# First weights, first rows and the tile search ahead of the branch: a perceiver block on one Trainium2 core

## The chip, the core and the metric

The kernel runs on one core of a Trainium2 chip. A core has five engines that run their own instruction lists and meet at semaphores: PE (TensorE, products), DVE (VectorE), ACT (ScalarE), POOL (GpSimd) and SP (SyncE, which here only issues transfers). Transfers between memory and the core run on DMA queues. The metric is the device time of one launch in microseconds (us): before the change 1093.79 us, the median of three runs that lay between 1090.33 and 1094.54.

## The reference

There are 32 items of 64 rows of width 512 (`x`), and for each a context of 1601 rows with a mask that marks the rows past the item's length. Three blocks follow each other, each on a layer norm of `x` and added to it:

```python
# 1. cross attention, 4 query heads, one key/value head of width 128; the query's rows are rms-normed again
xn, mn = rmsnorm(layernorm(x), rms_scale), rmsnorm(ctx, rms_scale)
q = rope(xn @ q_w) * 128 ** -0.5 ; k = rope(mn @ kv_w[0]) ; v = mn @ kv_w[1]
x = x + softmax(where(mask, q @ k.T, -2.38e38)) @ v @ out_w      # True keeps a context row
# 2. causal self attention, 16 heads of width 32
x = x + attn(layernorm(x), WQ, WK, WV, WO)
# 3. feed forward 512 -> 2048 -> 512, both weights rounded to -1, 0, 1; gelu and a layer norm between
x = x + (layernorm(gelu(layernorm(x) @ q(W_fc).T)) * ln_w + ln_b) @ q(W_proj).T
```

`mask` is True for the padding at the end of an item's context, and the reference keeps just the True rows, so of 1601 context rows an item needs 400 at most. Factors `1 + rms_scale` are folded into `q_w` and `kv_w`.

## The kernel before

**A plan, then a branch.** Context rows come in tiles of 128. `plan_tiles` finds for each item which tiles hold kept rows: transfers bring the mask to the core, DVE reduces it per tile, forms running sums and from them, per item, four row offsets, a flag (`pl[4]`: the kept rows fit four tiles) and a count of tiles. Beside it the mask's rows are gathered by an indirect transfer on POOL (L153) and stored as `kept_mask`. All five engines read `onepath` and branch: to `few` (four tiles an item, taken with these inputs) or to `every`.

**Which queue does what ahead of the branch.** SP issues the loads of the first operands (`dma0`, L311): the identity, both halves of `kv_w`, `rms_scale` (element by element), the first 128 rows of `x`, the four heads of `q_w`, two tables. All transfers of the search stand on ACT's queue (L115), the store of `kept_mask` too, and ACT branches behind it.

**Behind the branch.** `few` writes its instructions by a table of slots: each stage is entered with a slot and an order in it (`at`), and the slots are run off in order, which fixes each engine's list. Every list is worked off strictly in order. Products of full precision are made from two parts: the operand rounded (hi, by ACT) and the remainder (lo, by DVE), three products each; so weights are first scaled and split (L382 on ACT, L384 on DVE). For each pair of items, `stage_Q0` normalizes 128 rows of `x` (statistics on DVE L607 and L608, two inverse square roots on POOL L262 to L615), `stage_Q1` applies it (DVE L620), `stage_Q1b` transposes and splits it, `stage_Q2` forms the queries (12 products of 128x512, called Q2 below) with the rotary factors on DVE, `stage_Q3` transposes them. For each context tile k, T(k) is its transposes (PE L220) with their split (ACT L231, DVE L234), and KV(k) the 12 products of 128x256 that follow (PE L245).

**The order that matters here.** On PE: the transposes of the first rows, Q2, T(0), T(1), the transposes of Q, T(2), KV(0), T(3), KV(1), T(4), KV(2), T(5), KV(3), then the transposes of the second pair's normalized rows, T(6), KV(4). On DVE the statistics of the second pair's rows stand ahead of the remainder of tile 3. On POOL the bias of item 0, made from `kept_mask` (L669), stands ahead of the inverse square roots of the second pair. On SP, behind the branch: for items 0, 1 and 2 four context tiles and four tables each (24 transfers, the row offset of each context tile read from `picked`), then the second pair's rows of `x`, then `kept_mask` (both L196). Below, this sequence on SP is the train.

Of the kernel before, what the change touches and what calls it, by code (L numbers as in the profile page):

```python
# [7 lines left out]
F32 = mybir.dt.float32  # L8
# [3 lines left out]
I32 = mybir.dt.int32  # L12
# [20 lines left out]
class Sem:  # L33

    def __init__(self, handle):
        self.h, self.n = handle, 0
# [48 lines left out]
def plan_tiles(nc, handle, base, mask, tmask, kmask, places, seq, plan, picked, onepath):  # L86
# [4 lines left out]
    Q = Queues()  # L91
    sems = {}

    def sem(name):
        if name not in sems:
            sems[name] = Sem(handle(name))
        return sems[name]

    op = Q.op
# [11 lines left out]
    pl = tile("pl", [6], I32, 4)  # L111
# [5 lines left out]
    D_ = lambda f, waits=(): op("dve", f, sem("p_dve"), waits)  # L117
    P_ = lambda f: op("pool", f, sem("p_pool"))
    P_(lambda e: e.memset(mk[0:B, 0:128], 0))
    z = P_(lambda e: e.memset(mk[0:B, NT * 128:], 0))  # L120
    dma(mk[0:B, 128:NT * 128], mask[:, LAST:])
    dma(sq[0:B, :], seq)
    t = dma(mk[0:B, 0:LAST], mask[:, 0:LAST], [z])
    P_(lambda e: e.memset(c0[0:B, 0:8], 0.0))
    z = P_(lambda e: e.memset(c1[0:B, 0:8], 0.0))
    for k in range(FT):
        z = P_(lambda e, k=k: e.memset(tn[0:B, k:k + 1], float(k)))
    tm = dma(tmask.rearrange("b t k -> b (t k)"), mk[0:B, :], [t, z])
    v = D_(lambda e: e.tensor_reduce(c0[0:B, 8:], mk[0:B, 0:1664].rearrange("p (t k) -> p t k", t=NT),
                                     AX.X, ALU.max), [t, z])  # L130
    for n in range(4):
# [21 lines left out]
    g = op("pool", lambda e: e.indirect_dma_start(  # L153
        km[:, :], None, tmask.rearrange("b t k -> (b t) k"), bass.IndirectOffsetOnAxis(pi[:, 0:1], 0)),
        sem("p_rows"), [wp, tm], 16)
# [3 lines left out]
    return Q, rows  # L159

def few(nc, handle, bank, base, x1d, x2d, x, ctxd, mask, rms, qw, kvw, ow, WQ, WK, WV, WO, Wfc, lnw, lnb,
        Wproj, cosk, sink, cosq, sinq, identd, causald, out, picked, kmask, ktab, t_rows, nb=B):
# [4 lines left out]

    def sem(name):
        if name not in sems:  # L170
            sems[name] = Sem(handle(name))
        return sems[name]

    Q, Q0 = Queues(), Queues()

# [17 lines left out]
    op = Q.op  # L193
# [62 lines left out]
    t_id = Q0.op("sp", lambda e: e.dma_start(ident[:, :], identd), sem("s_id"), (), 16)  # L256
# [65 lines left out]
    t_rt = dma0(sq_t[:, :], sinq, "s_rt")
    loaded = (len(sems), [t_id, t_wkv, t_rms, t_xq0, t_wq, t_rt])
# [2178 lines left out]
```

How the kernel before makes its waits and increments, by code:

```python
    def op(self, eng, fn, sem=None, waits=(), inc=1):  # L48
        for w in waits:
            if w is None:
                continue
            s, v = w
            if self.seen[eng].get(s, 0) < v:
                self.seen[eng][s] = v
                self.q[eng].append(lambda e, s=s, v=v: e.wait_ge(s.h, v))
        if sem is None:
            self.q[eng].append(fn)
            return None
        self.q[eng].append(lambda e: fn(e).then_inc(sem.h, inc))
        sem.n += inc
        return (sem, sem.n)
# [7 lines left out]
        def f(e):  # L69
            with e.If(when()):
                for g in fns[:-1]:
                    g(e)
                fns[-1](e).then_inc(sem.h, 1)
            with e.Else():
                e.drain().then_inc(sem.h, 1)
# [267 lines left out]
        def g(e):  # L343
            with e.If(when()):
                f(e).then_inc(s.h, 16)
            with e.Else():
                e.sem_inc(s.h, 16)
# [2076 lines left out]
        def run(name, e):  # L2424
            early.play(name, e)
            first.play(name, e)
            fits = e.value_load(onepath[0:1, 0:1], min_val=0, max_val=1)
            with e.If(fits > 0):
                short.play(name, e)
            with e.Else():
                for s, n in [rows, *loaded[1]]:
                    e.wait_ge(s.h, n)
                long.play(name, e)
```

## Time and profile before

| | |
|---|---|
| three timed runs, us | 1093.79, 1090.33, 1094.54 |
| profiled execution, us | 1089.65 |
| its span on the core, us | 1087.8 |
| busy share of the span | PE 86%, DVE 62%, ACT 46%, POOL 34% |
| mean granted TensorE clock | 0.965 |

The span runs from the first to the last instruction that the profiler sees; the 1.85 us between it and the execution's time lie around it. Times in the rows below count from the span's start. A busy share is an average: PE is 86% busy over the whole, but in the first slice of 40 (27.2 us) it does not work at all, and that stretch is the one that the change touches.

### The profile page before, as it was taken

Reading aid. Unit: us, or ns where it says so; the run is one execution under the profiler, and the core shown is the slowest. Engines: PE = TensorE matmul, PEld = TensorE weight load, DVE = VectorE, ACT = ScalarE, POOL = GpSimd, SP = SyncE. Lnnn points to the kernel's source line nnn. Section 1 sums busy time; section 2 is a strip of 40 time slices with the busy share of each in tenths; the row PEclk is TensorE's granted clock in tenths of the full one; section 3 lists DMA queues with packets and bytes.
Section 4 is the critical chain, followed back from the end, with each engine's and each line's share of the span. In section 5 each row is a group of like instructions: output and inputs, shape, how many; then the busy total and the mean of one; then the engine's idle time right before and its main releaser. Section 6 shows DMA issues by size and latency. Waiting matters only on the chain.

```text
span 1087.8 us, 22528 instructions
## 1 busy us (share of the span) xinstructions
PE 931.0 (86%) x7297; PEld 697.5 (64%) x7297; DVE 669.2 (62%) x1335; ACT 503.0 (46%) x1057; POOL 373.1 (34%) x500
## 2 busy tenths in 40 slices
PE   0898879898788888868879989998978999999995
PEld 0787757686667776657768878887754444444442
DVE  3587667766677766676266556766565447475543
ACT  2565445654455554535233233443445444556551
POOL 1354445444444444430012111221112334454533
PEclk9999999999999999979969999999988989999997
DMA  5532133221232322431355543443321202012011
GB/s 163 167 87 65 58 95 97 87 63 48 81 89 77 88 70 75 112 101 60 79 156 147 137 146 88 139 125 116 97 46 48 68 1 87 31 39 68 20 59 42
DMA packets 100608, 93.02 MB, mean 86 GB/s; under 512 B 45729, under 2 KB 62194, under 8 KB 100466
## 3 DMA queue, kind: packets, MB, share of 16 engines
q1 hardware_dynamic: 99856, 91.11, 28.9%
q8 instruction: 73, 1.20, 0.5%
q14 instruction: 69, 0.57, 0.2%
q10 hardware_dynamic: 578, 0.13, 0.1%
q0 software_dynamic: 32, 0.02, 0.0%
HBM read 74.37 MB, written 12.66 MB: 80 GB/s over the span
## 4 chain that ended last, share of the span: by engine, by line
PE 65%; DVE 14%; issue 10%; ACT 5%; ACTq 1%; DVEq 1%; POOL 1%; DMA 1%; SPq 1%; POOLq 0%
PE bank L245 44%; PE bank L1216 8%; PE bank L220 6%; PE bank L241 4%; DVE f L234 3%; DVE f L508 2%; ACT f L231 1%; DVEq L75 1%; ACTq L75 1%; PE bank L530 1%; ACT f L413 1%; DVE f L471 1%; DVE f L642 1%; DVE f L929 1%; PE bank L216 1%
## 5 line engine op out<-in xcount | busy, mean ns | idle before, releaser
L245 PE MATMUL bank<-f,f 128*128 128x256 f32 (+4 forms) x5032 | 635.4, 302 | 67.9 <-issue 26.3
L245 PEld LDWEIGHTS bank<-f,f 128*128 128x128 f32 (+3 forms) x5032 | 457.5, 162 | 195.7 <-issue 77.2
L220 PE MATMUL bank<-f,f 128*128 128x128 f32 x896 | 133.4, 280 | 60.1 <-DVE f L620 29.3
L234 DVE TENSOR_TENSOR f<-bank,f 128x512 fp32r<-128x512 f32 x211 | 140.7, 684 | 52.6 <-ACT f L231 50.6
L231 ACT ACTIVATE f<-bank 128x512 fp32r<-128x512 f32 x211 | 121.2, 592 | 85.6 <-PE bank L220 80.5
L220 PEld LDWEIGHTS bank<-f,f 128*128 128x128 f32 x896 | 103.6, 143 | 82.8 <-DVE f L620 31.1
L1194 POOL TENSOR_TENSOR f<-f,f 128x512 f32<-128x512 f32 x60 | 76.4, 1274 | 146.6 <-ACT f L1192 146.5
L1216 PE MATMUL bank<-f,f 128*128 128x512 f16 x512 | 124.9, 389 | 0.0
L1197 DVE SCALAR_TENSOR_TENSOR f<-bank,f,f 128x512 f16<-128x512 f32 x64 | 48.0, 750 | 107.0 <-ACT f L1184 73.5
L935 POOL TENSOR_TENSOR f<-f,f 128x512 f32<-128x512 f32 x32 | 33.4, 1045 | 182.8 <-DVE f L932 182.8
L469 POOL TENSOR_TENSOR f<-f,f 128x512 f32<-128x512 f32 x32 | 42.0, 1312 | 155.9 <-ACTq L75 133.2
L1216 PEld LDWEIGHTS bank<-f,f 128*128 128x128 f16 x512 | 51.0, 100 | 64.0 <-issue 6.8
L1183 ACT ACTIVATE bank<-bank 128x512 f32<-128x512 f32 x64 | 37.2, 582 | 94.9 <-PE bank L245 94.9
L264 POOL TENSOR_TENSOR f<-f,f 128x1 f32<-128x1 f32 (+1 forms) x100 | 75.0, 750 | 8.3
L262 POOL TENSOR_SCALAR f<-f 128x1 f32<-128x1 f32 (+1 forms) x100 | 21.3, 213 | 147.0 <-DVE f L839 94.4
L519 ACT ACTIVATE f<-f,f 128x512 f32<-128x512 f32 x64 | 46.3, 724 | 50.2 <-DVE f L517 40.3
L883 ACT ACTIVATE f<-bank 128x256 f32<-128x256 f32 x64 | 24.4, 382 | 80.8 <-PE bank L245 80.2
L241 PE MATMUL bank<-f,f 128*128 128x256 f32 x372 | 53.1, 290 | 7.5 <-issue 4.7
L508 DVE CUSTOM_DVE_ANT_0 f<-bank,f 128x512 f32<-128x512 f32 x64 | 44.2, 690 | 24.5 <-PE bank L245 16.5
L231 ACT ACTIVATE f<-f 128x256 fp32r<-128x256 f32 (+1 forms) x52 | 25.3, 497 | 69.8 <-DVE f L566 69.4
L241 PEld LDWEIGHTS bank<-f,f 128*128 128x128 f32 x372 | 46.6, 190 | 13.5 <-issue 13.3
L413 ACT ACTIVATE f<-f 128x512 bf16<-128x512 f32 x71 | 44.0, 620 | 3.2 <-ACT f L413 2.2
(128 smaller groups left out, 989.0 us busy)
## 6 DMA issues: line engine op xcount, KB each, us to landing
f<-in_ctx_dram SPq DMA_DIRECT2D x71, 256.0 KB, 2.8
f<-x_scratch SPq DMA_DIRECT2D x64, 256.0 KB, 3.7
f<-in_x_dram SPq DMA_DIRECT2D x32, 256.0 KB, 3.2
x_scratch<-f SPq DMA_DIRECT2D x32, 256.0 KB, 2.1
f<-in_L_ffn_W_fc_dram SPq DMA_DIRECT2D x32, 256.0 KB, 2.8
f<-in_L_ffn_W_proj_dram SPq DMA_DIRECT2D x32, 256.0 KB, 3.5
f<-in_ktab_dram SPq DMA_DIRECT2D x71, 64.0 KB, 2.0
f<-f SPq DMA_DIRECT2D x64, 64.0 KB, 2.4
```

What stands on the lines that cost most here:

```text
L220: f = lambda e, i=i, a=a: e.transpose(dst[:, i, :], a, ident[0:rows, 0:rows])
L231: return maybe("act", lambda e: e.activation(hi, src, ACT.Copy), sem(name + "_hi"), waits, when)
L234: return maybe("dve", lambda e: e.tensor_tensor(lo, src, hi.bitcast(F32), ALU.subtract), sem(name + "_lo"), waits, when)
L241: fns = [lambda e, i=i, a=a, b=b: e.matmul(dst, a, b, start=(first and i == 0), stop=(last and i == n - 1), skip_group_check=True) for i, ...
L245: f = lambda e, i=i, a=a, b=b: e.matmul(dst, a, b, start=(first and i == 0), stop=(last and i == n - 1), skip_group_check=check)
L264: return op("pool", lambda e: e.tensor_tensor(dst, tmp, mhalf[0:dst.shape[0], 0:n], ALU.pow), sem(name + "_p"), [t])
L413: done["sq"] = maybe("act", lambda e: e.activation(sq[:, :], cx[:, b % NG, t, :], ACT.Square, accum_out=ss[:, b % 4, t:t + 1]), sem("s_ss" ...
L508: to = op("dve", lambda e: e.tensor_tensor_reduce(Pm[:, b % 2, t, :], bank[NL][:, :], bias[:, b % 2, :], 1.0, -3.0e38, ALU.add, ALU.max, m ...
L519: te = op("act", lambda e: e.activation(Pm[:, u, t, :], Pm[:, u, t, :], ACT.Exp, bias=nm[:, u, t:t + 1], accum_out=den[:, u, t:t + 1]), se ...
L1194: tp = op("pool", lambda e: e.tensor_tensor(acc[:, v, 1, :], acc[:, v, 1, :], sq3[:, z, :], ALU.add), sem("f_acc2"), [ts, *tok["acc2", g]])
L1197: tl = op("dve", lambda e: e.scalar_tensor_tensor(Gl[:, y, :], gp, lsc[:, 0, f:f + 1], Gh[:, y, :], ALU.mult, ALU.subtract), sem("f_G_lo") ...
L1216: fn = lambda e, t=t, v=v, G=G: e.matmul(bank[kp[t]][:, :], G[:, y, t * 128:(t + 1) * 128], WPb[:, f, :], start=(f == 0 and v == 0), stop= ...
```

## The change

Four things, all ahead of or at the branch:

1. The search's loads go to SP's queue, first of all there; `rms_scale` and the first rows of `x` go to ACT's queue. The later transfers of the search (`places`, `pi`, the gather, `kept_mask`) are issued by POOL.
2. `plan` and its two transfers go away. DVE multiplies the plan by the identity (`dg`, 32 partitions of 32x6), PE sums over the partitions by one product with a column of ones, and DVE copies the row to `picked`.
3. Of `few`, the scaling and splitting of `kv_w` and `q_w` and the first pair's `stage_Q0`, `stage_Q1` and `stage_Q1b` stand ahead of the branch (`Q0` before the search's own steps, `Q1` behind them). These use one semaphore an engine. The +1 on `rms_scale` goes from DVE to POOL.
4. The branch waits for the search's answer alone, no longer for its transfers. `few` and `every` share semaphores whose counts go on from where the part ahead left them.

```diff
 def plan_tiles(...):
-    def dma(dst, src, waits=()):
-        return op("act", lambda e: e.dma_start(dst, src), sem("p_dma"), waits, 16)
+    load = lambda dst, src, waits=(): QA.op("sp", lambda e: e.dma_start(dst, src), sem("p_mk"), waits, 16)
...
-    w = dma(plan, pl[0:B, :], [v])
-    wp = dma(places, pn[0:B, :], [vp])
-    w = dma(picked[0:1, :], plan.rearrange("(a b) k -> a (b k)", a=1), [w, wp])
-    wp = dma(pi[:, :], places.rearrange("b (t a) -> (b t) a", a=1).bitcast(U32), [w])
+    v = D_(lambda e: e.tensor_tensor(dg[0:B, :, :], pl[0:B, :].unsqueeze(1).to_broadcast([B, B, 6]),
+                                     ident[0:B, 0:B].unsqueeze(2).to_broadcast([B, B, 6]), ALU.mult), [v, t_id])
+    w = QB.op("pe", lambda e: e.matmul(bank[0:1, 0:6 * B], one[0:B, 0:1], dg[0:B, :, :].rearrange("p b k -> p (b k)"),
+                                       start=True, stop=True), sem("p_pe"), [v, z])
+    vp = D_(lambda e: e.tensor_tensor(pn[0:B, :], num[0:B, :], sq[0:B, :], ALU.add), [v1, t])
+    w = D_(lambda e: e.tensor_scalar(picked[0:1, :], bank[0:1, 0:6 * B], 1.0, None, ALU.mult), [w])
     fits = picked[0:1, :].rearrange("p (b k) -> p b k", b=B)[:, :, 4]
-    v = D_(lambda e: e.tensor_reduce(onepath[0:1, 0:1], fits, AX.X, ALU.min), [w, tm])
+    v = D_(lambda e: e.tensor_reduce(onepath[0:1, 0:1], fits, AX.X, ALU.min), [w])
+    wp = QB.op("pool", lambda e: e.dma_start(places, pn[0:B, :]), sem("p_pl"), [vp], 16)
+    wp = QB.op("pool", lambda e: e.dma_start(pi[:, :], places.rearrange("b (t a) -> (b t) a", a=1).bitcast(U32)),
+               sem("p_pl"), [wp], 16)
...
-    rows = dma(kmask.rearrange("b (t k) -> (b t) k", t=FT), km[:, :], [g])
+    rows = QB.op("pool", lambda e: e.dma_start(kmask.rearrange("b (t k) -> (b t) k", t=FT), km[:, :]),
+                 sem("p_km"), [g], 16)
     for eng in ("sp", "act", "pool", "pe", "dve"):
-        op(eng, lambda e: None, None, [v, w])
+        QC.op(eng, lambda e: None, None, [v])
 def few(...):
+    t_rms = dma0("act", rms1[:, :], rms.rearrange("(c p) -> p c", p=128), "s_e_rms", allow_slow_non_contiguous=True)
+    t_xq0 = dma0("act", xq[:, :], xf[0:128, :], "s_e_xq")
...
-    at(-12, -1, lambda: load_xq(0))
-    at(-12, 0, lambda: stage_Q0(0))
+    side[0] = Q0
+    t_r1 = op("pool", lambda e: e.tensor_scalar(rms1[:, :], rms1[:, :], 1.0, 1.0, ALU.mult, ALU.add), sem("r1"), [t_rms])
+    load_xq(0)
+    stage_Q0(0)
+    t_kvh = scaled_hi(wkv_t, Wkvh, [t_wkv, t_r1])
+    t_qh = scaled_hi(wq_t, WQh, [t_wq, t_r1])
+    side[0] = Q1
+    stage_Q1(0)
+    t_Wkv = scaled_lo(wkv_t, Wkvh, Wkvl, [t_wkv, t_r1], t_kvh)
+    stage_Q1b(0)
+    tw1["q"] = scaled_lo(wq_t, WQh, WQl, [t_wq, t_r1], t_qh)
+    side[0] = Q
     for c in range(4):
-        at(-11, 7, lambda c=c: stage_WQ(c))
         at(5 + c, 9, lambda c=c: stage_Wo(c))
 def program(...):
         def run(name, e):
-            early.play(name, e)
-            first.play(name, e)
+            for q in (steps[0], prep[0], steps[1], prep[1], steps[2]):
+                q.play(name, e)
             fits = e.value_load(onepath[0:1, 0:1], min_val=0, max_val=1)
```

ACT's list at its start, before: nine transfers of the search, the read of `onepath` and the branch, then the scalings (f_71 is the hi part of `kv_w`, f_67 of `q_w`) and squares of context rows (f_76).

```order
L115 DMA tile_plan<-pl 32x6
L115 DMA tile_rows<-pn 32x4
L115 DMA picked<-tile_plan 1x192
L115 DMA pi<-tile_rows 128x1
L115 DMA kept_mask<-km 128x128
L2427 TENSOR_LOAD onepath
L2427 ISA x2
L2428 COMPARE_AND_BRANCH
L382 ACT_TABLE_LOAD
L382 ACTIVATE f_71<-f_99,f_108 128x256 x4
L382 ACTIVATE f_67<-f_100,f_108 128x512 x4
```

The same place now (f_110 is `rms_scale`, f_84 the first rows of `x`, f_73 and f_69 the hi parts, f_86 that of the first pair's transposed rows):

```order
L322 DMA f_110<-in_L_xattn_rms_scale_dram 128x4x1
L322 DMA f_84<-in_x_dram 128x512
L668 ACT_TABLE_LOAD
L668 ACTIVATE f_73<-f_101,f_110 128x256 x4
L668 ACTIVATE f_69<-f_102,f_110 128x512 x4
L241 ACTIVATE f_86<-bank 128x512
L2447 TENSOR_LOAD onepath
L2447 ISA x2
L2448 COMPARE_AND_BRANCH
L407 ACTIVATE f_78,f_111<-f_68 128x512 x4
```

The search's nine transfers are gone from ACT, and its scalings and the first split stand ahead of its branch.

DVE's list, from the search's first steps to the first rows' normalization, before (f_82 is the first rows of `x`, f_72 and f_68 the lo parts):

```order
L129 TENSOR_REDUCE c_52<-mk 32x13
L145 SCALAR_TENSOR_TENSOR pl<-c_52,cnt 32x1
L146 TENSOR_TENSOR pn<-num,sq 32x4
L152 TENSOR_REDUCE onepath<-picked 1x1
L2427 TENSOR_LOAD onepath
L378 TENSOR_SCALAR f_108<-f_108 128x4
L384 SCALAR_TENSOR_TENSOR f_72<-f_99,f_108,f_71 128x256 x4
L607 BN_STATS f_116<-f_82 128x6
L608 BN_AGGR f_117<-f_116 128x2
L384 SCALAR_TENSOR_TENSOR f_68<-f_100,f_108,f_67 128x512 x4
L620 TENSOR_SCALAR f_83<-f_82,f_117,f_118 128x512
```

The same steps now (f_74 and f_70 the lo parts, f_87 that of the first rows):

```order
L601 BN_STATS f_118<-f_84 128x6
L602 BN_AGGR f_119<-f_118 128x2
L128 TENSOR_REDUCE c_54<-mk 32x13
L144 SCALAR_TENSOR_TENSOR pl<-c_54,cnt 32x1
L145 TENSOR_TENSOR dg<-pl,f_51 32x192
L150 TENSOR_SCALAR picked<-bank 1x192
L152 TENSOR_REDUCE onepath<-picked 1x1
L614 TENSOR_SCALAR f_85<-f_84,f_119,f_120 128x512
L673 SCALAR_TENSOR_TENSOR f_74<-f_101,f_110,f_73 128x256 x4
L244 TENSOR_TENSOR f_87<-bank,f_86 128x512
L673 SCALAR_TENSOR_TENSOR f_70<-f_102,f_110,f_69 128x512 x4
L2447 TENSOR_LOAD onepath
```

The statistics of the first rows now stand ahead of the search's first step, and everything down to the lo part of `q_w` ahead of DVE's branch. The orders named above for PE, DVE, POOL and SP behind the branch are the same in both kernels.

## Rows read from the trace of the kernel before

**Rows 1.** The page's first part: busy us, share of the span, instructions.

```profile
PE 931.0 (86%) x7297; PEld 697.5 (64%) x7297; DVE 669.2 (62%) x1335; ACT 503.0 (46%) x1057; POOL 373.1 (34%) x500
```

**Rows 2.** Chain of waits, opening: start us, us, what.

```profile
20.33 1.28 ACT L382
...
31.91 4.51 PE bank L245 x12
```

**Rows 3.** Timeline, DVE, search: start us, us, engine, line, operation [idle before].

```profile
4.87 1.88 DVE L129 TENSOR_REDUCE c<-mk 32x13 f32<-32x1664 uint8 x1 [4.87 <-DMA mk<-in_mask_BxS_bk_dram]
...
8.52 0.15 DVE L145 SCALAR_TENSOR_TENSOR pl<-c,cnt 32x1 int32<-32x1 f32 x1
...
13.13 0.20 DVE L152 TENSOR_REDUCE onepath<-picked 1x1 int32<-1x32 int32 x1 [4.38 <-DMA picked<-tile_plan]
```

**Rows 4.** Timeline, first issues on ACT's and SP's queues.

```profile
0.73 0.42 ACTq L115 DMA_DIRECT2D mk<-in_mask_BxS_bk_dram  x1
...
2.20 0.51 SPq L311 DMA_DIRECT2D f<-n_L_xattn_rms_scale_dram  x1
2.75 0.50 SPq L311 DMA_DIRECT2D f<-in_x_dram  x1
3.29 3.23 SPq L311 DMA_DIRECT2D f<-in_L_xattn_q_w_dram  x4
```

**Rows 5.** DMA issues: KB, us to landing; the last one issued about 4.9.

```profile
f<-n_L_xattn_rms_scale_dram SPq DMA_DIRECT2D x1, 2.0 KB, 5.1
f<-in_x_dram SPq DMA_DIRECT2D x1, 256.0 KB, 5.2
f<-in_L_xattn_q_w_dram SPq DMA_DIRECT2D x1, 256.0 KB, 6.2
```

**Rows 6.** Timeline, SP behind the branch: the train's first and last transfers.

```profile
15.03 3.63 SPq L361 DMA_DIRECT2D f<-in_ctx_dram  x4
...
34.17 0.43 SPq L196 DMA_DIRECT2D f<-in_x_dram  x1
34.65 0.43 SPq L196 DMA_DIRECT2D f<-kept_mask  x1
```

**Rows 7.** DMA issues of 34 to 35 us: KB, us to landing.

```profile
f<-in_x_dram SPq DMA_DIRECT2D x1, 256.0 KB, 2.9
...
f<-kept_mask SPq DMA_DIRECT2D x1, 64.0 KB, 4.3
```

**Rows 8.** Timeline, POOL, 39 to 46 us.

```profile
39.04 0.62 POOL L669 TENSOR_SCALAR f<-f 128x512 f32<-128x512 uint8 x1 [4.35 <-DMA f<-kept_mask]
42.59 0.19 POOL L262 TENSOR_SCALAR f<-f 128x1 f32<-128x1 f32 x1 [2.93 <-DVE f L608]
...
44.94 0.19 POOL L615 TENSOR_TENSOR f<-f 128x1 f32<-128x1 f32 x1
```

**Rows 9.** Timeline, DVE, the second pair's statistics and normalization.

```profile
41.60 0.69 DVE L607 BATCH_NORM_STATS2 f<-f 128x6 f32<-128x512 f32 x1
...
45.81 0.54 DVE L620 TENSOR_SCALAR f<-f,f,f 128x512 f32<-128x512 f32 x1
```

**Rows 10.** Timeline, PE: KV(3) and KV(4).

```profile
45.26 1.68 PE L245 MATMUL bank<-f,f 128*128 128x256 f32 x12
...
47.57 1.67 PE L245 MATMUL bank<-f,f 128*128 128x256 f32 x12
```

**Rows 11.** Windows: length, busy us (instructions) of PE, PEld, DVE, ACT, POOL; PEclk; DMA; GB/s.

```profile
472.00:474.00 2.00, 0.19 (x2) 0.22 (x2) 1.60 (x5) 0.30 (x1) 0.78 (x3) 1.00 0.03 9
...
476.00:478.00 2.00, 1.62 (x6) 1.35 (x6) 1.20 (x4) 0.73 (x3) 0.00 (x0) 0.50 0.03 8
```

**Rows 12.** Timeline, PE: 12 products of 128x512 at either clock.

```profile
443.11 2.91 PE L245 MATMUL bank<-f,f 128*128 128x512 f32 x12
...
483.95 5.38 PE L245 MATMUL bank<-f,f 128*128 128x512 f32 x12 [2.30 <-DVEq L75]
```

**Rows 13.** Groups by shape: busy us, mean ns; a full-precision product of 512 columns.

```profile
L1292 PE MATMUL bank<-f,f 6*128 6x512 f32 x4 | 2.6, 790 | 0.0
```

More of the change, by code:

```diff
@@ L33, with __init__ @@
 class Sem:
[L36 to L37 removed]
+    def __init__(self, handle, begun):
+        self.h, self.n = handle, begun
 class Queues:
@@ L83, in play, with plan_tiles @@
             f(e)
-def plan_tiles(nc, handle, base, mask, tmask, kmask, places, seq, plan, picked, onepath):
-    Q = Queues()
+def plan_tiles(nc, handle, base, ident, t_id, bank, mask, tmask, kmask, places, seq, picked, onepath):
+    QA, QB, QC = Queues(), Queues(), Queues()
     sems = {}
@@ L157, in plan_tiles @@
     for eng in ("sp", "act", "pool", "pe", "dve"):
-        op(eng, lambda e: None, None, [v, w])
-    return Q, rows
+        QC.op(eng, lambda e: None, None, [v])
+    return (QA, QB, QC), rows, [sems[k].n if k in ("p_pool", "p_dve", "p_pe") else None for k in sems]
 def few(nc, handle, bank, base, x1d, x2d, x, ctxd, mask, rms, qw, kvw, ow, WQ, WK, WV, WO, Wfc, lnw, lnb,
-        Wproj, cosk, sink, cosq, sinq, identd, causald, out, picked, kmask, ktab, t_rows, nb=B):
+        Wproj, cosk, sink, cosq, sinq, identd, causald, out, picked, kmask, ktab, plan, nb=B):
@@ L167, in few @@
     sems = {}
+    Q, Q0, Q1 = Queues(), Queues(), Queues()
+    side = [Q0]
     def sem(name):
+        if side[0] is not Q and not name.startswith("s_e"):
+            return "s_e"
         if name not in sems:
-            sems[name] = Sem(handle(name))
+            sems[name] = Sem(*handle(name))
         return sems[name]
-    Q, Q0 = Queues(), Queues()
     class Region:
@@ L192, in snapshot, with op @@
         return [(s, s.n) for s in sems.values() if s.n]
-    op = Q.op
+    def op(eng, fn, s=None, waits=(), inc=1):
+        return side[0].op(eng, fn, sem("s_e" + eng) if s == "s_e" else s, waits, inc)
     def dma(dst, src, s, waits=()):
@@ L255, in few @@
     ident, mhalf = const(128), const(16)
-    t_id = Q0.op("sp", lambda e: e.dma_start(ident[:, :], identd), sem("s_id"), (), 16)
+    t_id = Q0.op("sp", lambda e: e.dma_start(ident[:, :], identd), sem("s_e_id"), (), 16)
+    steps, t_rows, begun = plan(ident, t_id)
     t_mh = op("pool", lambda e: e.memset(mhalf[:, :], -0.5), sem("s_mh"))
@@ L670, in stage_mask, with scaled_hi, scaled_lo @@
             bias[:, u, :], msk[:, u, :], -FILL, FILL, ALU.mult, ALU.add), sem("s_bias"), [t, *d("lgo", b - 2)])]
-    at(-12, -1, lambda: load_xq(0))
-    at(-12, 0, lambda: stage_Q0(0))
+    def scaled_hi(src, hi, waits):
+        return [op("act", lambda e, c=c: e.activation(hi[:, c, :], src[:, c, :], ACT.Copy, scale=rms1[:, c:c + 1]),
+                   sem("hi"), waits) for c in range(4)]
+    def scaled_lo(src, hi, lo, waits, ths):
+        for c in range(4):
+            tl = op("dve", lambda e, c=c: e.scalar_tensor_tensor(
+                lo[:, c, :], src[:, c, :], rms1[:, c:c + 1], hi[:, c, :].bitcast(F32),
+                ALU.mult, ALU.subtract), sem("lo"), [ths[c], *waits])
+        return ths[-1], tl
+    side[0] = Q0
[10 more added lines that the diff above has]
+    side[0] = Q
+    ahead = [(s, s.n) for s in sems.values()]
+    begun = [*begun, *(None if k.startswith("s_e_") else s.n for k, s in sems.items())]
     for c in range(4):
-        at(-11, 7, lambda c=c: stage_WQ(c))
         at(5 + c, 9, lambda c=c: stage_Wo(c))
@@ L1348, in few @@
     op("sp", lambda e: None, None, snapshot())
-    return Q, Q0, loaded
+    return Q, (Q0, Q1), steps, [t_rows, *ahead], begun
 def every(nc, handle, bank, base, x1d, x2d, x, ctxd, mask, rms, qw, kvw, ow, WQ, WK, WV, WO, Wfc, lnw, lnb,
@@ L2430, in run @@
             with e.Else():
-                for s, n in [rows, *loaded[1]]:
+                for s, n in ahead:
                     e.wait_ge(s.h, n)
```

91 lines of the change are left out of this document (38 added, 53 removed).

## Prediction, made before the changed kernel was run

> **What bounds the kernel now.** I read the page first: PE is the busiest engine with 86% of the span [rows 1], so what counts after the opening is when PE's steady run of products begins; everything behind it moves with it. Then the chain of waits of the opening: it does not run through PE until Q2 at 31.91, and before that it stands on ACT, whose table load comes at 20.33 because ACT has first to issue the search's last transfer and to branch [rows 2]. The timeline gives the rest in three pieces. The search: DVE starts on the mask at 4.87, has the plan at 8.52 + 0.15 = 8.67, and then waits 4.38 for the plan's way through memory, so that the answer stands at 13.33 [rows 3]. The train on SP: first context transfer at 15.03, that is 1.70 behind the answer, then the 24 transfers, the second pair's rows of `x` at 34.17 and `kept_mask` at 34.65 [rows 6]: 19.14 and 19.62 behind the train's start. And what hangs on these two: they land 2.9 and 4.3 after their issue [rows 7]; POOL makes the bias at 39.04, having waited 4.35 for nothing but `kept_mask`, and only behind it the second pair's inverse square roots [rows 8]; these release DVE's normalization at 45.81 [rows 9], whose transposes stand ahead of KV(4) on PE [rows 10]. Before, this side chain was not late: POOL idled 2.93 between bias and roots, for DVE's statistics. It is what comes late next.
>
> **The change, part by part.**
>
> *The search's answer.* DVE now has the first rows' statistics ahead of the search, so the search waits for these rows. Before, the rows were issued at 2.75 and `rms_scale` ahead of them at 2.20 [rows 4], landing 5.2 and 5.1 later [rows 5], at 7.95 and 7.30. Now `rms_scale` is issued at 0.73, ACT's first issue [rows 4], and the rows some 0.5 later, at about 1.2. Bounds: 1.2 + 2.9 = 4.1, by a lone transfer of the same size [rows 7], and 1.2 + 5.2 = 6.4, by the slow landing of before. The element-by-element `rms_scale` is still ahead of them and the weights still share the way, so I take 6.1, near the upper end. The Trainium skill (DMA: Bandwidth & Descriptors, Issuing engines are not separate DMA queues) says that transfers of several issuing engines run on the same 16 DMA engines and interleave, so that a second issuer saves only the issue time; by it the landing would stay at 6.4, by the lone row it would be 4.1. Statistics of 512 columns take 0.69 [rows 9], with the small operation behind them about 0.9, an estimate: the search starts at 7.0 instead of 4.87. Its DVE steps are the same, 8.67 - 4.87 = 3.80, so the plan stands at 10.8. Then come a multiplication of 192 columns, about 0.35 (from 0.15 for one column [rows 3] and 0.69 for 512 [rows 9]); the product, 0.79 x 192/512 = 0.30 at the full clock [rows 13] and twice that at half, since PE has done nothing so far; the copy, 0.35; the minimum, 0.20 [rows 3]; four handovers of about 0.05. That is 1.7 instead of 4.66, and the answer stands at 12.5: 0.8 earlier than before. Ends: rows at 4.1 give 10.5, 2.8 earlier; rows that land no sooner than before, at 7.95, give 14.3, 1.0 later.
>
> *ACT and DVE ahead of the branch.* The last transfer of `q_w` was issued at about 4.9 and landed 6.2 later, at 11.1 [rows 5]. Now three small loads stand ahead on SP and two have left it; call it 12. Behind it, one after the other, stand four hi parts on ACT, the split of the first rows (hi on ACT, lo on DVE) and four lo parts on DVE: ten passes of 512 columns at some 0.69 [rows 9], 6.9. Q2 starts near 19 instead of 31.91. Alone that is worth 13. The answer at 12.5 and the rows' normalization behind it are hidden under the weights' landing.
>
> *POOL's transfers.* The gather's chain is now issued by POOL alone, behind the answer's inputs at 10.8. The nearest rows are the landings of rows 7, 2.9 to 4.3: four in turn end between 22 and 28, and `kept_mask` is asked for only near 34. POOL's own branch falls into the same stretch, and its first work behind it is due with KV(1). I count nothing.
>
> *The train.* It is not shortened: same 24 transfers, same order. It moves with the answer, 0.8. So the second pair's rows land at 34.17 - 0.8 + 2.9 = 36.3, and `kept_mask` at 34.65 - 0.8 + 4.3 = 38.2. With Q2 near 19, KV(0), KV(1), KV(2) would be done near 32 (Q2 to KV(3): 45.26 - 31.91 = 13.35 before [rows 2, 10]). Then DVE stands at the statistics of rows that are not there, with the lo part of tile 3 behind them, and PE waits some 5 us. From the bias on: 38.25 + 0.62 + 2.54 (42.59 to 44.94 + 0.19 [rows 8]) = 41.4; normalization 0.54 = 41.95; and 1.22 from its end to KV(4), as before (45.81 + 0.54 to 47.57 [rows 9, 10]) = 43.2. KV(4) was at 47.57: the gain is 4.4 there. What follows (rope, key transposes, later items) hangs on the same engines in the same order, and context loads of items 3 and on are free earlier, so I carry 4.4 to the end.
>
> *The clock.* PE's wait of 5 us has a price. In this trace PE worked 0.19 of 2 us from 472 on, and from 476 its granted clock read 0.50, the 1.2 GHz level [rows 11]; 12 products of 512 columns then took 5.38 instead of 2.91 [rows 12], so 2.5 per dozen and half of it, 1.2, per dozen of 256 columns. KV(3) can pay this for nothing, as it ends before 41.95; KV(4) and the transposes ahead of it pay up to 1.7 if the level has not come back. I take 0.5, between 0 and 1.7. The Trainium skill (TensorE: Matmul & The Clock Gate, Part 1) says the same of the direction: idle time lowers the clock and only sustained work brings it back; by it the waiting PE would pay the upper end on KV(4), by the rows KV(3) may already have restored the level.
>
> *Sum.* The profiled execution took 1089.65; 4.4 less and 0.5 more gives 1085.75. The median of the runs is 1093.79, 4.1 above that execution, which would make it 1089.9. The four executions lie within 5 us; I put the time at 1088.9, between the two.
>
> **The rivals.**
>
> *Early answer.* The first rows land near 4.1 and the answer at 10.5, or `kept_mask` lands in the 2.9 of its neighbour, since less is in flight: 2.0 to 3.4 more than above, a gain of 6 to 8 and 1086. For it: nothing but a small load is ahead on ACT's queue. Against: 5.1 for that small load.
>
> *Full carry.* The opening moves by the 13 of Q2, to 1080. It needs the second pair's rows and `kept_mask` 8 earlier than the train brings them. Nothing in the order of SP, DVE or POOL allows it, unless the train was held by transfers in flight and not by its own issues; 0.8 an issue (19.14 for 24) with a landing of 2.9 behind it [rows 6, 7] does not look like that.
>
> *Half clock.* PE, idle near 32, drops to 1.2 GHz, and the following thin stretch does not bring it back. The price is 1.2 a tile. From the fourth tile at the low level on (4.9) the gain is gone; for 5.5 slower than before it takes eight tiles, 1099. For it: the drop of rows 11. Against: the first products behind an idle opening, Q2's, took 4.51 and not 5.38 [rows 2, 12], so the level came back within them.
>
> *It does not do what it says.* The rows land at 7.95, the answer is late by 1.0, so is the train: gain 2.6 less the clock, 1091.5. This I count with the forecast.
>
> **How the numbers follow.** Medians of three runs that lie 4 apart tell about 0.5%, 5.5 us, from no change. Forecast, a gain of 2 to 6 held by the train: 0.62, of which 0.15 is beyond 5.5 by its spread; its own range is 1086 to 1092. Early answer: 0.27, nearly all of it faster. Full carry: 0.05, faster. Half clock: 0.06, of which 0.03 is slower by more than 5.5. So faster 0.15 + 0.24 + 0.05 = 0.44, slower 0.03, the same 0.53. The range that leaves out the full carry and the long spell of half clock is 1083.5 to 1094.
>
> **What would show it.** The answer near 12.5 and the train's first issue near 14.2; Q2 near 19; a wait of some 5 us on PE ahead of KV(3), put down to DVE; POOL's bias released by `kept_mask` near 38.2; KV(4) near 43. I am wrong if KV(4) starts before 40 or after 46, if POOL is waited for through its own transfers, or if the difference between the two traces at the end is not the one at KV(4).

## The result, and the profile of the changed kernel

The changed kernel takes 1084.81 us (median of seven runs, 1081.18 to 1085.96), the kernel before, with more runs on the same chip, 1091.21 (median of seven, 1089.26 to 1094.54). The ratio is 0.9929 with an interval of [0.991, 0.9948]: faster by 0.7%, and the whole interval lies, just, beyond the 0.5% that counted as no change. The profiled execution took 1082.82 with a span of 1081.0, against 1089.65 and 1087.8. The forecast, 1088.9 and no change as the likeliest outcome, was wrong. The rival called "early answer" is what happened.

The opening on DVE, from the timeline (start, duration, engine, line, operation, idle time before it). It answers to [rows 3]:

```profile
4.25 0.69 DVE L601 BATCH_NORM_STATS2 f<-f 128x6 f32<-128x512 f32 x1 [4.25 <-DMA f<-in_x_dram]
...
5.08 1.87 DVE L128 TENSOR_REDUCE c<-mk 32x13 f32<-32x1664 uint8 x1
...
8.56 0.14 DVE L144 SCALAR_TENSOR_TENSOR pl<-c,cnt 32x1 f32<-32x1 f32 x1
8.73 0.34 DVE L145 TENSOR_TENSOR dg<-pl,f 32x192 f32<-32x192 f32 x1
...
9.97 0.35 DVE L150 TENSOR_SCALAR picked<-bank 1x192 int32<-1x192 f32 x1 [0.81 <-PE bank L147]
10.35 0.20 DVE L152 TENSOR_REDUCE onepath<-picked 1x1 int32<-1x32 int32 x1
```

The statistics wait for the first rows until 4.25 only, so the search starts 0.2 later than before (5.08 against 4.87), although it now stands behind them. The plan is there at 8.70 and the answer at 10.55, 1.85 behind it. Before it was 13.33: the answer is 2.78 earlier.

The reason is in the landings (issues between 0 and 3 us: tile, queue, KB, us from issue to landing), against [rows 5]:

```profile
f<-in_x_dram ACTq DMA_DIRECT2D x1, 256.0 KB, 3.0
...
f<-n_L_xattn_rms_scale_dram ACTq DMA_DIRECT2D x1, 2.0 KB, 2.2
```

Both took about 5 before. Behind the branch SP's train follows as it did (timeline of SP, first and last transfers, against [rows 6]):

```profile
12.22 3.64 SPq L371 DMA_DIRECT2D f<-in_ctx_dram  x4
...
31.41 0.43 SPq L206 DMA_DIRECT2D f<-in_x_dram  x1
31.89 0.43 SPq L206 DMA_DIRECT2D f<-kept_mask  x1
```

The first transfer is 2.81 earlier, the last two 2.76: the 24 transfers take 19.19 instead of 19.14. What hangs on the last two, on POOL and then on DVE, against [rows 8, 9]:

```profile
35.26 0.63 POOL L663 TENSOR_SCALAR f<-f 128x512 f32<-128x512 uint8 x1 [13.29 <-DMA f<-kept_mask]
35.96 0.19 POOL L273 TENSOR_SCALAR f<-f 128x1 f32<-128x1 f32 x1
```

```profile
34.76 0.69 DVE L601 BATCH_NORM_STATS2 f<-f 128x6 f32<-128x512 f32 x1 [7.66 <-DMA f<-in_x_dram]
...
35.59 1.25 DVE L244 TENSOR_TENSOR f<-bank,f 128x512 fp32r<-128x512 f32 x2
38.54 0.55 DVE L614 TENSOR_SCALAR f<-f,f,f 128x512 f32<-128x512 f32 x1 [1.70 <-POOL f L609]
```

POOL's pause of 2.93 between the bias and the roots is gone, as the prediction had it: the roots start at 35.96, right behind the bias. DVE stands 7.66 at the statistics, and the two lo parts of the context tiles queued behind them come late. PE (timeline, against [rows 10]) shows what that does:

```profile
16.55 5.27 PE L255 MATMUL bank<-f,f 128*128 128x512 f32 x12 [4.38 <-DVE f L673]
...
28.80 1.68 PE L255 MATMUL bank<-f,f 128*128 128x256 f32 x12
36.39 1.08 PE L230 MATMUL bank<-f,f 128*128 128x128 f32 x4 [5.92 <-DVE f L244]
37.13 2.91 PE L255 MATMUL bank<-f,f 128*128 128x256 f32 x12
39.83 1.91 PE L230 MATMUL bank<-f,f 128*128 128x128 f32 x8
41.39 1.93 PE L255 MATMUL bank<-f,f 128*128 128x256 f32 x12
...
55.56 2.38 PE L255 MATMUL bank<-f,f 128*128 128x256 f32 x15
```

Q2 starts 15.4 earlier, KV(2) ends at 30.48, and then PE waits for the lo part of the next context tile. KV(4) starts at 41.39, 6.18 earlier than before. The 15 products at 55.56 stood at 61.48 before, so 5.92 are left there, and 6.8 at the end of the span. KV(3) took 2.91 instead of 1.68. The windows (length, busy us and instructions of PE, PEld, DVE, ACT, POOL, granted clock, DMA share, GB/s) say why:

```profile
30.00:36.00 6.00, 0.47 (x4) 0.27 (x3) 1.21 (x3) 1.19 (x4) 0.67 (x2) 0.93 0.73 209
36.00:42.00 6.00, 5.61 (x27) 5.64 (x28) 3.04 (x6) 2.51 (x6) 4.31 (x10) 0.51 0.90 285
42.00:50.00 8.00, 8.00 (x59) 7.46 (x59) 5.80 (x10) 4.40 (x12) 3.79 (x5) 1.00 0.36 106
```

PE worked 0.47 us of six; in the next six its granted clock read 0.51, the 1.2 GHz level, and from 42 on 1.00 again.

`kept_mask` lands sooner (DMA issues of 31 to 32.5 us), against [rows 7]:

```profile
f<-kept_mask SPq DMA_DIRECT2D x1, 64.0 KB, 3.3
```

And one line of DVE from the kernel before (timeline), which stood right ahead of its normalization in [rows 9]:

```profile
45.20 0.69 DVE L234 TENSOR_TENSOR f<-bank,f 128x512 fp32r<-128x512 f32 x1 [2.09 <-ACT f L231]
```

So the gain at KV(4) adds up, each piece the difference of two rows. The bias starts 3.78 earlier: 2.76 by `kept_mask`'s issue, 1.02 because it landed 3.3 instead of 4.3 behind it. POOL's pause of 2.93 has shrunk to 0.07, which is 2.86, and from the roots to the normalization it is 2.58 instead of 3.22, another 0.64, since before the normalization stood behind the lo part at 45.20, while POOL was done at 45.13. Together the normalization starts 7.27 earlier (45.81 to 38.54). From the normalization's end to KV(4) it is 2.30 instead of 1.22, so 1.08 go back. That makes 6.2. Less than half of it is the answer's 2.8.

These pieces follow the normalization, which ends at 39.09. PE is busy with KV(3) until 40.04, so the normalization had 0.95 to spare, and the chain of waits that ended last runs through the second pair's rows and KV(3):

```profile
31.41 3.32 DMA f<-in_x_dram
...
37.47 2.56 PE bank L255 x12
```

So of the 1.0 by which `kept_mask` landed sooner KV(4) has little: without it the normalization would end about when KV(3) does. Why it landed sooner is not shown. It is not the early answer: in the version below whose answer comes 4.9 later it took 3.4. Nor was less in flight: the transfers moved 204, 233 and 250 GB/s in the three stretches of 2 us from 31 on, against 169, 124 and 6 from 34 on before.

### The profile page after: what moved, and what is told of

The parts are those of the page before. It is cut to its first block, busy times and chain, and to the rows that moved or that the text cites. A ratio compares the mean times of both kernels' runs of the same rounds, so it can differ in the third digit from the quotient of the medians.

```text
span 1081.0 us, 22531 instructions
## 1 busy us (share of the span) xinstructions
PE 934.9 (86%) x7299; PEld 700.5 (65%) x7299; DVE 669.5 (62%) x1336; ACT 503.4 (47%) x1057; POOL 374.8 (35%) x505
## 4 chain that ended last, share of the span: by engine, by line
PE 65%; DVE 14%; issue 9%; ACT 5%; SPq 2%; ACTq 1%; DVEq 1%; DMA 1%; POOL 1%; POOLq 0%
PE bank L255 44%; PE bank L1234 8%; PE bank L230 6%; PE bank L251 4%; DVE f L244 3%; DVE f L502 2%; ACT f L241 1%; DVEq L75 1%; ACTq L75 1%; PE bank L524 1%; ACT f L407 1%; DVE f L465 1%; DVE f L947 1%; PE bank L226 1%; DVE f L636 1%
## 5 line engine op out<-in xcount | busy, mean ns | idle before, releaser
L502 DVE CUSTOM_DVE_ANT_0 f<-bank,f 128x512 f32<-128x512 f32 x64 | 44.2, 690 | 24.7 <-PE bank L255 16.8
```

The source lines that it names most:

```text
L502: to = op("dve", lambda e: e.tensor_tensor_reduce(Pm[:, b % 2, t, :], bank[NL][:, :], bias[:, b % 2, :], 1.0, -3.0e38, ALU.add, ALU.max, m ...
```

## Experiments

Two questions were open: whether the train really sets what is gained (theory 1), and not Q2 or PE's clock; and why the first rows landed so soon. All edits are to the changed kernel; ratios are to the kernel before.

### The second pair's rows alone, earlier in the train

```diff
-                at(s0 - 12, 1.4, lambda i=i: load_xq(i))
+                at(*((s0 - 12, 1.4) if i > 1 else (-11, 1.7)), lambda i=i: load_xq(i))
```

The load goes behind item 0's tables, 8 transfers into the train.

> The changed kernel, with the load of the second pair's rows moved up in SP's train: behind item 0's tables instead of behind item 2's. kept_mask stays last. Theory 1 (the train: KV(3) waits for these rows and KV(4) for kept_mask, both at the train's end): the rows are there before they are needed, KV(3) starts near 30.7 instead of 37.1 without a wait, but the bias still waits for kept_mask (about 35.7) and KV(4) stays at 40.5 to 41.5 (41.39 in the changed kernel); time within 1 us of 1084.8. Theory 2 (only the rows gate, the bias is hidden): KV(4) near 32.5, time near 1076. Theory 3 (nothing of the train gates, the earlier Q2 set the gain): no change anywhere.

1085.66 (median of four), ratio 0.9936 [0.9916, 0.9956]: no gain over the changed kernel's 0.9929. The wait was not removed, it moved by one tile (PE, timeline):

```profile
30.87 1.68 PE L255 MATMUL bank<-f,f 128*128 128x256 f32 x12
39.92 1.97 PE L230 MATMUL bank<-f,f 128*128 128x128 f32 x8 [7.37 <-DVE f L614]
41.54 2.91 PE L255 MATMUL bank<-f,f 128*128 128x256 f32 x12
```

KV(3) now runs on at full clock, but the transposes of the second pair's normalized rows wait 7.37, since POOL's bias, waiting for `kept_mask` until 36.05, still stands ahead of the roots. PE's granted clock reads 0.50 from 36 to 46, and the 15 products come at 57.48, 1.9 later than in the changed kernel.

### `kept_mask` alone, earlier in the train

```diff
+    def load_first_mask():
+        early_mask[0] = load_mask(0)
...
-        t = load_mask(b)
+        t = early_mask[b] if b in early_mask else load_mask(b)
...
+    at(-11, 2.55, load_first_mask)
```

The load stands behind item 1's context tiles.

> The changed kernel, with kept_mask asked for behind item 1's context tiles instead of last; the second pair's rows stay at the train's end. Theory 1: the bias is made near 27 and gates nothing, but the rows land near 35.2 and DVE's statistics hold KV(3) as before; KV(3) near 37, KV(4) within 0.6 of 41.39, time within 1 us of 1084.8. Theory 2 as in the run with the rows moved: no change, since the rows still gate. A theory that kept_mask alone gates: KV(4) near 33, time near 1076.

1083.84 (median of four), 0.9919 [0.9898, 0.994]: again like the changed kernel. Now POOL stands ready and waits for the statistics, whose rows still come at the train's end, and PE waits as before:

```profile
35.73 0.19 POOL L273 TENSOR_SCALAR f<-f 128x1 f32<-128x1 f32 x1 [8.91 <-DVE f L602]
```

```profile
36.36 1.09 PE L230 MATMUL bank<-f,f 128*128 128x128 f32 x4 [6.29 <-DVE f L244]
```

### Both earlier

Both edits together.

> The changed kernel with both moved up: the second pair's rows behind item 0's tables, kept_mask behind item 1's context tiles. Theory 1: no wait of PE ahead of KV(3), KV(3) near 30.7, KV(4) near 33, so 8 less than 41.39, carried to the end: 1076 to 1077. Theory 3: no change, 1084.8. A theory that the gain of the opening is lost again further on (context tiles of items 1 and 2, which come 0.5 to 1 later now): KV(4) near 33, but the end within 3 us of 1084.8.

1079.81 (median of six), 0.9896 [0.9876, 0.9915]. The wait is gone and KV(4) starts at 32.11, 9.3 earlier than in the changed kernel. The interval of its times still overlaps with that of `kept_mask` alone, so it is these 9.3 that carry the finding. Two edits that are each worth nothing are worth some 4 together: the side chain needs both transfers, and the train ends with both. That is theory 1, shown. But the time stayed some 3 above the expected 1076 to 1077, and PE and ACT show where it went:

```profile
32.11 1.67 PE L255 MATMUL bank<-f,f 128*128 128x256 f32 x12
...
49.88 1.94 PE L230 MATMUL bank<-f,f 128*128 128x128 f32 x8 [7.30 <-DVE f L244]
51.47 2.64 PE L255 MATMUL bank<-f,f 128*128 128x256 f32 x12
...
54.31 2.37 PE L255 MATMUL bank<-f,f 128*128 128x256 f32 x15
```

```profile
45.68 0.63 ACT L241 ACTIVATE f<-f 128x512 fp32r<-128x512 f32 x1 [9.15 <-DMA f<-in_L_xattn_out_w_dram]
```

A second wait of the same kind: ACT stands 9.15 at the split of `out_w`, which nobody needs yet, and the context tiles behind it come late. `out_w` is 1 MB, was issued at 37.59 and took 8.1 to land. At 54.31 only 1.25 of the 9.3 are left against the changed kernel. Its span is 4.4 shorter; the other 3.1 lie behind that point. By the starts of the same products in the two traces, 1.1 of them arise right behind it, where PE in the changed kernel waits 0.86 for DVE at 61.09, and most of the rest between 745 and 940, where the granted clock reads 0.94 on average against 0.92. That this second part comes from the edit is not shown.

### The weights' preparation behind the branch again

```diff
     stage_Q0(0)
+    side[0] = Q1
     t_kvh = scaled_hi(wkv_t, Wkvh, [t_wkv, t_r1])
...
-            for q in (steps[0], prep[0], steps[1], prep[1], steps[2]):
+            for q in (steps[0], prep[0], steps[1], steps[2]):
...
             with e.If(fits > 0):
+                prep[1].play(name, e)
                 short.play(name, e)
             with e.Else():
+                prep[1].play(name, e)
```

The scalings, the lo parts, and the first rows' application, transposes and split go behind the branch in both of its arms; the early loads, the statistics and the product stay.

> The changed kernel with the parts of kv_w and q_w and the application, transposes and split of the first rows behind the branch again (on ACT, DVE and PE); the statistics, the search's product, the queues and the roots on POOL stay as changed. Theory 1 (the train gates): Q2 near 21.3 instead of 16.55, KV(0) near 29.7 instead of 25.06, but KV(3) still waits for rows that land at 34.7, so KV(4) is at 40.3 to 41.4 and the time within 1.5 us of 1084.8: the preparation ahead of the branch is worth nothing here. Theory 3 (the earlier Q2 is what carried the gain): 4.7 later from Q2 to the end, 1089.5.

1082.22 (median of six), 0.991 [0.9895, 0.9925]: no slower. Q2 starts at 20.77 instead of 16.55, and yet KV(4) comes 1.4 earlier than in the changed kernel:

```profile
20.77 5.30 PE L255 MATMUL bank<-f,f 128*128 128x512 f32 x12 [7.60 <-DVE f L673]
...
33.06 1.68 PE L255 MATMUL bank<-f,f 128*128 128x256 f32 x12
...
35.95 0.63 PE L230 MATMUL bank<-f,f 128*128 128x128 f32 x4 [1.22 <-DVE f L244]
36.34 1.67 PE L255 MATMUL bank<-f,f 128*128 128x256 f32 x12
...
39.96 1.68 PE L255 MATMUL bank<-f,f 128*128 128x256 f32 x12
```

PE reaches the train's end later, waits 1.22 instead of 5.92, and KV(3) and KV(4) run at full clock. The chain of waits that ended last runs through `kept_mask` (issued at 31.79, 3.37 to landing), POOL and the normalization here. The largest part of the change, by its instructions, is worth nothing where it stands: it makes PE early for a wait, and the wait costs it the clock.

### The two first loads behind `kv_w` on SP again

```diff
-    t_rms = dma0("act", rms1[:, :], ...)
-    t_xq0 = dma0("act", xq[:, :], xf[0:128, :], "s_e_xq")
     for v in range(2):
         t_wkv = dma0("sp", wkv_t[:, :, v * 128:(v + 1) * 128], ...)
+    t_rms = dma0("sp", rms1[:, :], ...)
+    t_xq0 = dma0("sp", xq[:, :], xf[0:128, :], "s_e_xq")
```

> The changed kernel with one part undone: rms_scale and the first rows go out on SP's queue again, behind kv_w and ahead of q_w. If the place of these two loads decided the answer: they land some 5 after their issue as before the change (rows near 9.3 instead of 4.25), the statistics end near 10.2, the answer stands near 15.7 instead of 10.55, the train starts 5 later, KV(4) is near 46.5 instead of 41.39, the time near 1090: nearly the whole gain is gone although everything else of the change is in. If the place does not matter (the rows would land within 3 of their issue at about 4.1): answer near 13.4, KV(4) near 44.3, 1087.5.

1088.49 (median of ten), 0.9984 [0.997, 0.9998]: nearly the whole gain is gone. The loads, issued at 3.60 and 4.16, took 4.9 and 5.0 (DMA issues from 3 to 5 us), and all behind them moved:

```profile
f<-in_x_dram SPq DMA_DIRECT2D x1, 256.0 KB, 5.0
...
f<-n_L_xattn_rms_scale_dram SPq DMA_DIRECT2D x1, 2.0 KB, 4.9
```

```profile
9.15 0.69 DVE L601 BATCH_NORM_STATS2 f<-f 128x6 f32<-128x512 f32 x1 [9.15 <-DMA f<-in_x_dram]
...
15.25 0.20 DVE L152 TENSOR_REDUCE onepath<-picked 1x1 int32<-1x32 int32 x1
```

The answer stands at 15.45, 4.90 later than in the changed kernel, and KV(4) at 46.41, 5.02 later. So what is lost at the answer arrives at KV(4) one for one. Yet KV(4) is still 1.16 earlier than before the change (47.57), with an answer 2.12 later than there: POOL's pause between the bias and the roots is gone here too (0.08 instead of 2.93).

### The same loads on ACT's queue, but behind the weights

SP issues the weights first, and ACT's two loads wait for the identity matrix, so that they start amid the weights' traffic on a queue of their own.

```diff
-        return Q0.op(eng, lambda e: e.dma_start(dst, src, **how), sem(s), (), 16)
+        return Q0.op(eng, lambda e: e.dma_start(dst, src, **how), sem(s), [t_id] if eng == "act" else (), 16)
...
-            for q in (steps[0], prep[0], steps[1], prep[1], steps[2]):
+            for q in (*((prep[0], steps[0]) if name == "sp" else (steps[0], prep[0])), steps[1], prep[1], steps[2]):
```

> A measurement, not a version: SP issues the weights first and the mask's loads last, and ACT issues rms_scale and the first rows on its own queue once the identity has landed (about 3.0), so that they set out while the weights are in flight, as they did before the change, but not behind them in one queue. If the slow landing of before (5.1 and 5.2) was the queue's order: rms_scale lands 2.2 to 3.0 after its issue and the rows 3.0 to 3.5. If it was the traffic of the weights on whatever queue: near 5 again for both. The search is late in either case (mask near 10), so KV(4) and the time are those of before or worse and say nothing.

The landings (DMA issues of 0 to 8 us):

```profile
f<-in_x_dram ACTq DMA_DIRECT2D x1, 256.0 KB, 5.4
...
f<-n_L_xattn_rms_scale_dram ACTq DMA_DIRECT2D x1, 2.0 KB, 4.8
```

Issued at 2.60 and 3.13 on ACT's own queue they are as slow as on SP's. So it is not the queue, and not the element-by-element form of `rms_scale`, which landed in 2.2 in the changed kernel. What differs there for these two loads is that the weights set out first, at 1.17: it is what is already in flight. (1087.94, one run; the mask's loads come late in it, so its time says nothing of the change.)

### The plan through memory again

```diff
-    v = D_(lambda e: e.tensor_tensor(dg[0:B, :, :], ...), [v, t_id])
-    w = QB.op("pe", lambda e: e.matmul(bank[0:1, 0:6 * B], ...), sem("p_pe"), [v, z])
...
-    w = D_(lambda e: e.tensor_scalar(picked[0:1, :], bank[0:1, 0:6 * B], 1.0, None, ALU.mult), [w])
+    w = QB.op("sp", lambda e: e.dma_start(plan, pl[0:B, :]), sem("p_mem"), [v], 16)
+    w = QB.op("sp", lambda e: e.dma_start(picked[0:1, :], plan.rearrange("(a b) k -> a (b k)", a=1)), sem("p_mem"), [w], 16)
```

> The changed kernel with the plan going through memory again instead of through the product (store and load both on SP, no identity product, no copy). Price of that part alone by the rows of before: 4.66 from the plan to the answer instead of 1.85 (8.70 to 10.55), so the answer near 13.4, the train 2.8 later, KV(4) near 44.2, time near 1087.6. If the answer's time does not carry over to KV(4): KV(4) at 41.4 and 1084.8.

1084.72 (median of nine), 0.9957 [0.9941, 0.9973]. The way takes 3.91 (8.56 to 12.47) instead of 1.85:

```profile
8.42 0.14 DVE L144 SCALAR_TENSOR_TENSOR pl<-c,cnt 32x1 int32<-32x1 f32 x1
...
12.27 0.20 DVE L149 TENSOR_REDUCE onepath<-picked 1x1 int32<-1x32 int32 x1 [3.64 <-DMA picked<-tile_plan]
```

The answer is 1.92 later than in the changed kernel and KV(4), at 43.03, 1.64: the product is worth that. I had expected an answer at 13.4 and KV(4) at 44.2 because I had taken the 4.66 of before for the way through memory; on SP, with these rows, it took 3.91. The medians are alike (1084.72 here, 1084.81 there), and the intervals of the two ratios, 0.9957 and 0.9929, overlap, so it is the trace that carries this.

### Both earlier, and `out_w` later

The edits of "both earlier", and

```diff
-        at(5 + c, 9, lambda c=c: stage_Wo(c))
-    at(3, 9, load_wo)
+        at(13 + c, 9, lambda c=c: stage_Wo(c))
+    at(4, 2, load_wo)
```

> The kernel with rows and kept_mask moved up in the train (KV(4) at 32.1 there, but a second wait of 7.3 on PE behind out_w, whose 1 MB lands 8.1 after its issue and is split far ahead of its use), and besides: out_w is loaded behind the third pair's rows and split eight slots later. Theory: no wait of PE over 1.5 between 25 and 55, the first three products of scores near 47 instead of 54.3 (58.1 in the changed kernel's count of 15 products at 55.56), so 8 to 9 below the changed kernel: 1075 to 1077. Rival: the next load of the train takes the wait's place and the time stays at 1080.

1076.15 (median of five), 0.9865 [0.9839, 0.9891], as expected. It beats both kernels: its interval lies wholly below the changed kernel's; it touches that of "both earlier" (0.9876 to 0.9891), against which the trace shows the difference. PE runs through the opening:

```profile
16.69 5.32 PE L255 MATMUL bank<-f,f 128*128 128x512 f32 x12 [4.66 <-DVE f L678]
...
33.19 1.67 PE L255 MATMUL bank<-f,f 128*128 128x256 f32 x12
...
46.15 2.38 PE L255 MATMUL bank<-f,f 128*128 128x256 f32 x15
```

Its window from 25 to 55 us (columns as in the windows above) has PE busy for 29.38 of 30 us, at the full clock:

```profile
25.00:55.00 30.00, 29.38 (x233) 28.07 (x233) 22.88 (x39) 21.32 (x54) 16.23 (x28) 1.00 0.63 187
```

The 15 products stand at 46.15, 8.2 earlier than with "both earlier" and 15.3 earlier than in the kernel before, and the span is 13.5 shorter. So the 15.2 that Q2 has gained here (31.91 to 16.69) reach the 15 products whole, once nothing else is late. Behind them a part goes: PE waits 1.21 for DVE at 69.74, and its granted clock reads 0.83 from 80 to 90. The load and the split of `out_w` were moved together; which of the two does it was not separated.

### The same, with the preparation behind the branch

The edits of the two experiments "both earlier, and `out_w` later" and "the weights' preparation behind the branch" together.

> The version with rows, kept_mask and out_w moved in the train (1076.15, ratio to before 0.9865, KV(4) at 33.19), and in it the parts of kv_w and q_w and the application, transposes and split of the first rows behind the branch again, the same edit that cost nothing in the changed kernel (KV(4) 39.96 there against 41.39). Theory: the preparation ahead of the branch is worth what the train does not gate; with the train's gates gone it is worth the shift of Q2, 4.2 (20.77 against 16.55): Q2 near 20.9, KV(4) near 37.4, about 1080.3, ratio 0.990. Rival: the preparation is worth nothing wherever it stands (something else, as the context tiles, sets KV(4)): KV(4) near 33 to 34 and 1076.

1079.28 (four runs, 1075.63 to 1080.74), 0.9905 [0.9881, 0.9928]. Q2 comes at 20.73 instead of 16.69 and KV(4) at 36.22 instead of 33.19:

```profile
20.73 4.32 PE L255 MATMUL bank<-f,f 128*128 128x512 f32 x12 [7.60 <-DVE f L678]
...
33.91 1.68 PE L255 MATMUL bank<-f,f 128*128 128x256 f32 x12
...
36.22 1.67 PE L255 MATMUL bank<-f,f 128*128 128x256 f32 x12
```

That is 3.0 at KV(4), not the expected 4.2: Q2 starts 4.04 later, but its 12 products took 4.32 instead of 5.32. Between the medians, which come from two chips, it is 3.1. The intervals touch (0.9881 to 0.9891), so the trace shows the 3.0 and the times only agree with it. So the preparation is worth something where the train no longer stands behind it, and in the changed kernel, where it does, nothing.

## Why the prediction was wrong

**The train sets the gain: right.** The 24 transfers kept their 19.2, started 1.67 behind the answer (forecast 1.70), and the second pair's rows and `kept_mask` carried the rest. The experiments that moved the answer (4.90 at the answer, 5.02 at KV(4); 1.92 and 1.64) and those that took both transfers out of the train's end show it from both sides. "Full carry" was rightly put low: of Q2's 15.4 the wait of 5.92 and the low clock behind it left 6.2 at KV(4), and experiment and forecast agree on its place, PE ahead of KV(3), released by DVE. One reading was off, at no cost to the sum: POOL's roots did not release the normalization at 45.81 before, since they were done at 45.13 and a lo part stood between; the 2.54 of the sum was 2.58.

**The landing of the first rows: the step that failed.** The prediction put the landing at 6.1, between 4.1 and 6.4, near the upper end "by the slow landing of before". It was 4.25. From there on every DVE step is as foreseen: search 5.08 with 3.6 to the plan, and the way to the answer 1.85 (forecast 1.7). So the answer came at 10.55 and not 12.5, and the bias 2.99 before its forecast: 1.95 of it from the answer, 1.0 from `kept_mask`'s landing, which I had left at 4.3. The rival "early answer" had named both, the answer at 10.5 and the landing; its reason for the landing, that less is in flight, is not borne out, and the cause of this 1.0 stays open. The argument against that rival, 5.1 for a small load, was read as a property of that load. For `rms_scale` the runs show it as one of its surroundings: 2.2 ahead of the weights, 4.9 on SP and 4.8 on ACT behind the weights. The first weight is issued at 2.57, when `rms_scale` has been under way for 1.8 and the rows for 1.35.

On this I had weighed the Trainium skill (DMA: Bandwidth & Descriptors, Issuing engines are not separate DMA queues): a transfer that another engine starts runs on the same 16 DMA engines and interleaves with the rest. The rule holds here, as ACT's 4.8 and 5.4 amid the weights show. My use of it was wrong: it speaks of transfers that are in flight together, and I had not asked what was in flight between 0.7 and 2.6.

**The product: right in place, nearly in size.** 1.85 for 1.7. The product itself took 0.79 on PE at the beginning of the program, not the 0.60 that I had taken for half clock.

**The preparation: right that it carries nothing, wrong in its date.** Q2 came at 16.55, not 19, since `q_w` was there for ACT at 9.99 (I had taken its last part at 12). That made PE's wait longer (5.92 against 5), and the run without the early preparation shows KV(4) 1.4 earlier for it.

**POOL's transfers: right.** `kept_mask` is stored by POOL from 19.43 on, and asked for at 31.89. Nothing waits for the gather.

**The clock: the right mechanism, half the size.** I took 0.5 between 0 and 1.7; it is 1.08, the growth of the stretch from the normalization to KV(4), and another 0.26 goes by the 15 products (6.18 to 5.92), since KV(4) itself took 1.93 instead of 1.67. The forecast had let KV(3) pay for nothing because it would end before the normalization. It ends at 40.04, the normalization at 39.09: PE was still at the low level when the rows were ready. The runs that shortened PE's wait to 1.22, or took it away, kept the full clock there, so wait and clock go together here. The longer low spell of the rival "half clock" did not come; the clock read 1.00 from 42 on.

**The level.** In its own execution's terms I had 1089.65 - 3.9 = 1085.75, and 1082.82 was measured: 2.9 of the miss. At KV(4) it is 2.3 (6.2 instead of 4.4 less 0.5): 1.95 of it is the early answer, and `kept_mask`'s 1.0 and the 0.6 by which the clock cost more nearly cancel there. The other 0.6 arises behind KV(4), and its cause is open. The last 1.2 of the miss is the 3.15 by which I went up towards a median of three runs; the changed kernel's median is only 2.0 above its profiled execution. One sum is off, and nothing hangs on it: for the rival "It does not do what it says", 1.8 behind the forecast's 1088.9 is 1090.7, not 1091.5. Of what the prediction named as its refutation nothing came: KV(4) lies between 40 and 46, POOL's transfers are not waited for, and the end's difference, 6.8, is the 6.2 of KV(4) and little more. The mechanism held; two landings in it did not, that of the first rows above all.

## What to carry to other kernels

In these runs the landing time of a load at the start went with what was in flight at that moment, not with the transfer: for a load that moves to another time, take the row with the same traffic around it, not the row with the same shape. In a list of transfers that one engine issues in order, look at its last entries first; what is gained ahead of it can be lost there, and an entry that is needed sooner goes ahead by one number in the schedule. Take such waits away in groups: each of two late inputs hides the other, and a third may stand behind them.

## What was not expected of the hardware

The spread between executions of one kernel goes largely with the mean granted clock. The seven of the changed kernel read, as mean clock and time: 0.966 and 1081.18; 0.963 and 1083.59; 0.961 and 1082.82; 0.958 and 1085.05, 1085.96; 0.957 and 1084.81, 1084.83. Between the ends lie 0.009 and some 4 us. It is no rule: of the five with "both earlier, and `out_w` later" the one with the highest clock, 0.966, is the slowest, 1078.07. So a difference of 2 to 4 between two medians says little of an edit in the first 60 us; there the starts of single products tell it. The last pair of runs is such a case: KV(4) is 3.0 later in the second, but its profiled execution, at 0.969, took 1075.63 against 1076.16 of the first at 0.963. The first has a stretch at the low level that the second has not (from 80 to 90 us 0.83 against 1.00); what sets such stretches off is not shown.

The granted clock's record seems not to cover the program's beginning. The window from 0 to 25 of the changed kernel reads 1.00, and so does that from 0 to 4, where PE does nothing, while Q2's 12 products took 5.27, against 2.91 and 5.38 at either level in [rows 12]: near the low one, by that comparison.
